# A deformable convolution and a top-2 mixture of experts on one core: the expert stage in two parts of 28 and 4 bands, with blocks of 128 rows

## The reference, cut to what matters

```
x = x + deformable_conv(layernorm_c(x))     # 3x3 taps, offsets and mask from a 3x3 convolution
t = tokens(x)                               # 4096 tokens of 128 channels
xf = layernorm(t)
logits = xf @ gate_w + gate_b               # 8 experts
probs = softmax(logits);  top2_vals, top2_idx = top_k(probs, 2)
for e in experts:
    h = gelu(xf @ W1[e] + b1[e])            # 128 -> 256
    y = h @ W2[e] + b2[e]                   # 256 -> 128
    out += weight of e for the token (0 if not chosen) * y
x = t + out
```

## Time and profile before

| what | us |
|---|---|
| median of 3 runs (lowest to highest) | 394.06 (393.71 to 394.44) |
| the profiled execution: its own time | 396.24 |
| its span, from the first to the last instruction | 394.4 |
| PE, PEld busy | 307.0, 261.2 |
| DVE, ACT, POOL busy | 224.6, 203.4, 217.8 |
| mean granted TensorE clock | 0.913 of full |

### The profile page before, as it was taken

The page is one execution under the profiler, slowest core; times in us unless marked ns, Lnnn a source line. Parts: engine busy times, 40 slices in busy tenths (PEclk is TensorE's granted clock), DMA queues, the critical chain, the costliest instruction groups (busy, mean ns, idle before and its releaser), DMA issues.

```text
span 394.4 us, 9789 instructions
## 1 busy us (share of the span) xinstructions
PE 307.0 (78%) x2395; PEld 261.2 (66%) x2395; DVE 224.6 (57%) x988; ACT 203.4 (52%) x526; POOL 217.8 (55%) x319
## 2 busy tenths in 40 slices
PE   0999599999999999999999984069889887885000
PEld 0365388888898888898888873048767676775000
DVE  2974347888888888888888775402122221222085
ACT  1254557667667766766766750324434443432053
POOL 5012232576776767777777545206777777777300
PEclk9999869999999999999999997559999999999555
DMA  8948822222222222222222100654768777771397
GB/s 212 272 131 239 318 75 85 84 97 101 88 97 93 97 89 91 96 93 91 92 92 96 53 28 28 167 168 156 231 202 252 222 229 237 234 227 63 94 316 229
DMA packets 50345, 57.83 MB, mean 147 GB/s; under 512 B 6892, under 2 KB 37999, under 8 KB 50320
## 3 DMA queue, kind: packets, MB, share of 16 engines
q1 hardware_dynamic: 43824, 48.12, 38.7%
q0 software_dynamic: 4544, 8.44, 6.6%
q10 hardware_dynamic: 1952, 0.99, 1.2%
HBM read 30.66 MB, written 14.97 MB: 116 GB/s over the span
## 4 chain that ended last, share of the span: by engine, by line
PE 51%; SPq 16%; issue 10%; ACT 8%; DMA 8%; POOL 2%; DVE 2%; ACTq 2%; POOLq 0%; DVEq 0%
PE bank L1367 18%; PE bank L1357 16%; ACT samp L765 7%; SPq L490 5%; PE bank L1272 5%; SPq L499 4%; SPq L505 3%; PE bank L1306 3%; DMA wide<-result 2%; DMA w_blk<-w_all 2%; POOL result L665 2%; PE bank L1284 2%; DMA result<-y,to 1%; PE bank L1478 1%; SPq L542 1%
## 5 line engine op out<-in xcount | busy, mean ns | idle before, releaser
L665 POOL DMA_INDIRECT result<-y,to x78 | 76.8, 985 | 41.9 <-DVE to L1215 23.0
L1367 PE MATMUL bank<-filt_sb,samp 128*128 128x128 f32 x576 | 77.0, 282 | 5.9 <-ACT samp L765 4.7
L1357 PE MATMUL bank<-S,xwin 100*128 100x144 f32 x512 | 79.8, 307 | 0.1
L604 POOL DMA_INDIRECT routed<-payload,slot x64 | 64.5, 1007 | 25.7 <-issue 15.0
L1367 PEld LDWEIGHTS bank<-filt_sb,samp 128*128 128x128 f32 x576 | 70.1, 194 | 11.2 <-ACT samp L765 9.8
L1357 PEld LDWEIGHTS bank<-S,xwin 100*128 100x128 f32 x512 | 69.4, 194 | 8.4 <-issue 7.3
L1223 DVE TENSOR_TENSOR y<-bank,w_blk 128x256 f32<-128x256 f32 x39 | 16.6, 425 | 79.9 <-PE bank L1487 76.8
L736 ACT ACTIVATE ysp<-bank 100x512 f32<-100x512 f32 (+1 forms) x96 | 46.7, 487 | 26.8 <-PE bank L1306 25.3
L932 DVE TENSOR_TENSOR S<-ysp,bank 100x512 f32<-100x512 f32 (+1 forms) x96 | 53.0, 553 | 9.8 <-ACT ysp L736 3.8
L765 ACT ACTIVATE samp<-bank 128x432 f32<-128x432 f32 (+1 forms) x96 | 47.2, 492 | 20.4 <-PE bank L1357 19.3
L1478 PE MATMUL bank<-rowsT,w_blk 128*128 128x256 f32 x156 | 45.0, 413 | 15.6 <-DMA w_blk<-w_all 13.7
(11 more groups left out here) (109 smaller groups left out, 433.8 us busy)
## 6 DMA issues: line engine op xcount, KB each, us to landing
w_blk<-w_all SPq DMA_DIRECT2D x39, 321.0 KB
xwin<-lines SPq DMA_DIRECT2D x64, 120.0 KB
xwin<-lines SPq DMA_DIRECT2D x32, 160.0 KB
rows_in<-routed SPq DMA_DIRECT2D x39, 129.0 KB, 2.6
wide<-result SPq DMA_DIRECT2D x16, 256.0 KB, 4.7
w_all<-in_experts SPq DMA_DIRECT2D x4, 642.0 KB, 7.5
out_tiles<-res SPq DMA_DIRECT2D x8, 256.0 KB, 4.6
wide<-in_x_rows SPq DMA_DIRECT2D x3, 512.0 KB, 9.2
```

Of the source, the lines that this page charges most:

```text
L604: nc.gpsimd.indirect_dma_start(routed, bass.IndirectOffsetOnAxis(slot[:, par, c2:c2 + 1], 0), payload[:, q, c2, :], None).then_inc((s.scat ...
L665: nc.gpsimd.indirect_dma_start(result, bass.IndirectOffsetOnAxis(to[:, slot, j:j + 1].bitcast(U32), 0), y[:, slot, j, :], None, bounds_che ...
L1357: last = nc.tensor.matmul(bank[5 + (par + g) % 2][:, i * TAPS * TT:(i + 1) * TAPS * TT], xwin[:, q, t, :], weights[:, t], start=True, stop ...
L1367: last = nc.tensor.matmul(bank[7][:, 0:C], samp[:, par, j, :], filt_sb[:, order[j], :], start=(j == 0), stop=(j == TAPS - 1))
```

## The change

The tokens are divided into two parts, the first 28 bands and the last 4. Each part has its own half of every expert's region in `routed`, its own running count (`seen`, `seen2`), its own plan and its own paddings.

- Blocks have 128 rows (`BLOCK = P`). Part 0 has at most 63 of them and part 1 at most 15, 78 in all, in a straight list without a loop. A send is now one indirect DMA for each block, with the destinations read from `rows_in` itself; `keep_dest` and `to` are gone.
- Part 0 is counted by PE in band 30's step and planned by DVE in the steps of bands 30 and 31 (`plan`, 14 links; the plan is computed with one block per partition and turned by two small matmuls, `turn_plan`). Part 1 is planned between the blocks 3 and 14.
- SP writes all paddings, those of part 0 before the first block, those of part 1 after block 26. It fetches eight block rows at a time. Rows have 16 slots and are loaded four blocks ahead of the weights.
- SP's weight transfer carries W1, b1 and b2 only (386 floats for each of 128 partitions instead of 642), into six slots. PE reads W2 where it lies, in `w_all`, at an address from the expert's number, which it has from packed words (`load_words`).
- The last bands' steps hold the first blocks' instructions already.
- `y_back` has a place of its own for each of the eight groups. A token's number is now its partition times 32 plus its band, so that a group is loaded back by one DMA with 2 KB pieces. SP issues the loads of the first seven groups behind its last weight transfer; ACT issues the eighth. DVE combines in place in `x1`.

```diff
-BLOCK = 256
+BLOCK = P
+SPLIT = 28
+PART_BANDS = (SPLIT, BANDS - SPLIT)
...
-W_UP = HID + HALVES
-WROW = W_UP + HALVES * C + C
-RING = 4
+W_B2 = HID + HALVES
+W_KEPT = W_B2 + C
+WROW = W_KEPT + HALVES * C
+RING = 6
+ROWS_AHEAD = 4
+ROWS = 16
...
+PACK, PACK_BITS = 8, 3
...
             def load_weights(i, row):
+                slot = i % RING
                 expert = nc.s_assert_within(row >> REGION_BITS, 0, EXPERTS - 1)
                 at_least(sp, s.y_done, i - (RING - 1))
-                sp.dma_start(w_blk[:, slot, :], w_all[:, expert, :]).then_inc(w_arrived[slot], 16)
+                sp.dma_start(w_blk[:, slot, :], w_all[:, expert, 0:W_KEPT]).then_inc(w_arrived[slot], 16)
+            def load_rows(i, row):
+                slot, uses = i % ROWS, i // ROWS
+                at_least(sp, sent[slot], 16 * uses)
+                sp.dma_start(rows_in[:, slot, :], routed[bass.ds(row, BLOCK), :]).then_inc(rows_arrived[slot], 16)
...
+            write_paddings(0)
+            sp.wait_ge(s.idle_written, 16)
             sp.wait_ge(s.experts_loaded, 16 * (EXPERTS // 2))
             sp.wait_ge(s.plan_ready, 1)
+            rows = []
+            for i in range(BLOCKS + ROWS_AHEAD):
+                if i < BLOCKS:
+                    part, at = int(i >= FIRST_BLOCKS), i % FIRST_BLOCKS
+                    if i == FIRST_BLOCKS:
+                        sp.wait_ge(s.plan_ready, 2)
+                    if at % PACK == 0:
+                        rows += first_rows(part, at)
+                    if at == 0:
+                        part_written(part)
+                    load_rows(i, rows[i])
+                if i >= ROWS_AHEAD:
+                    load_weights(i - ROWS_AHEAD, rows[i - ROWS_AHEAD])
+                if i == 26:
+                    write_paddings(1)
+            all_sent(sp, FIRST_BLOCKS)
+            for g in range(FIRST_BACKS):
                 load_back(g)
+            for g in range(BACKS):
+                if g == FIRST_BACKS:
+                    all_sent(sp, BLOCKS)
+                sp.wait_ge(s.out_ready, g + 1)
+                sp.dma_start(out[:, g * GB:(g + 1) * GB, :], x1[:, g * GB:(g + 1) * GB, :]).then_inc(s.stored, 16)
...
                 scatter(BANDS - 2, 0, 2)
+                send(0)
                 scatter(BANDS - 1, 1, 3)
...
+            for i in range(1, BLOCKS):
+                send(i)
...
+            for i in range(2, BLOCKS):
+                gelu(i)
+                if i + 2 < BLOCKS:
+                    evacuate_rows(i + 2)
+                if i == 12:
+                    act.wait_ge(s.exp_in, 1)
+                    nc.scalar.activation(e_all[:, :, :], e_all[:, :, :], ACT.Exp).then_inc(s.exp_out, 1)
+                    gelu_table(3)
...
+            for g in range(BACKS):
+                if g == FIRST_BACKS:
+                    all_sent(act, BLOCKS)
+                    for h in range(FIRST_BACKS, BACKS):
+                        act.dma_start(y_back(h), result[0:2 * P * BANDS, :].rearrange(
+                            "(c p g b) d -> g p c (b d)", c=2, p=P, b=GB)[h]).then_inc(back_arrived[h], 16)
...
+                    if known and b == SPLIT + 2:
+                        for link in range(6):
+                            plan(0, link)
+                    if known and b == SPLIT + 3:
+                        plan(0, PLAN_LINKS)
+                        plan(0, PLAN_LINKS + 1)
                     normalise(b - 1, other, (q + 3) % QUEUED)
...
+            def down(i, expert):
+                slot = i % RING
+                pe.wait_ge(s.h_ready, i * HALVES + HALVES)
+                for h in range(HALVES):
+                    last = nc.tensor.matmul(moe_bank[slot][:, 3 * BLOCK:4 * BLOCK], hid[:, slot, h, :],
+                                            w_all[:, expert, W_KEPT + h * C:W_KEPT + (h + 1) * C],
+                                            start=(h == 0), stop=(h == HALVES - 1))
+                last.then_inc(s.y_psum2, 1)
...
+            for i in range(3, BLOCKS):
+                if i == 12:
+                    turn_plan(1, BANDS)
+                if i == 40:
+                    experts_of += load_words(pe, mybir.EngineType.PE, 1, 0, SECOND_WORDS)
+                up(i)
+                if i + 2 < BLOCKS:
+                    transpose_rows(i + 2)
+                down(i - 1, experts_of[i - 1])
+            down(BLOCKS - 1, experts_of[BLOCKS - 1])
```

More of the change, by code:

```diff
@@ L327, in settle @@
             eng.sem_inc(s.settled, 1)
[L330 to L343, removed]
-                step(TURNS, place)
@@ new lines, in program, with y_back, all_sent @@
+        back_arrived = (s.back_0, s.back_1, s.back_2, s.back_3, s.back_4, s.back_5, s.back_6, s.back_7)
+        w_arrived = (s.w_in_0, s.w_in_1, s.w_in_2, s.w_in_3, s.w_in_4, s.w_in_5)
+        def y_back(g):
+            return y_first[:, g] if g < 4 else y_more[:, g - 4]
+        def all_sent(eng, blocks):
+            for slot in range(ROWS):
+                eng.wait_ge(sent[slot], 16 * len(range(slot, blocks, ROWS)))
+        PLAN_LINKS = 12
+        moe_bank = (bank[0], bank[1], bank[2], bank[3], bank[5], bank[6])
@@ L361, in program, with load_words @@
+        def load_words(eng, kind, part, first, end):
+            eng.wait_ge(s.experts_loaded, 16 * (EXPERTS // 2))
+            eng.wait_ge(s.words_ready, part + 1)
+            _, held = nc.values_load_multi_w_load_instructions(
+                words[0:1, part, first:end], engines=[kind], min_val=0, max_val=(1 << PACK * PACK_BITS) - 1)
+            return [(word >> PACK_BITS * at) & (EXPERTS - 1) for word in held for at in range(PACK)]
         x_arrived = (s.x_in_0, s.x_in_1, s.x_in_2, s.x_in_3)
@@ L369, in rows_of, with part_of @@
             return ap.rearrange("(one o) -> one o", one=1).broadcast_to([P, n])
-        def write_paddings(eng, kind, first, n):
-            _, rows = nc.values_load_multi_w_load_instructions(
-                pad_row[0:1, first:first + n], engines=[kind], min_val=0, max_val=(EXPERTS - 1) * REGION + P * BANDS)
-            for row in rows:
-                eng.dma_start(routed[bass.ds(row, BLOCK), :].rearrange("(p j) w -> p j w", j=PAD_RUN),
-                              padding_sb[:, :, :].bitcast(F32)).then_inc(s.pads_written, 16)
+        def part_of(b):
+            return 1 if isinstance(b, int) and b >= SPLIT else 0
         def is_far(eng):
@@ L847, in _ @@
[L847 to L857 removed]
+                evacuate_rows(0)
@@ L964, in _, with choose @@
             CHAIN = 6
-            def choose(b, par, link):
+            DVE_KIND = mybir.EngineType.DVE
+            def choose(b, par, link, part=None):
                 if no_band(b):
                     return
+                ranks = (seen, seen2)[part_of(b) if part is None else part]
                 if link == 0:
@@ L1122, in step @@
                         multiply(b, par, 2)
+                    if known and b == SPLIT + 3:
+                        for link in range(6, PLAN_LINKS):
+                            plan(0, link)
                     residual(b - 1, other, 0)
@@ L1231, in _ @@
[L1231 to L1248 removed]
+                finish(1)
@@ L1251, in _ @@
+            for g in range(BACKS):
+                combine(g)
         @block.tensor
```

613 lines of the change are left out of this document (317 added, 296 removed).

## The result

| | before | after |
|---|---|---|
| median (lowest to highest) | 394.25 (393.71 to 394.98, 4 runs) | 419.07 (416.96 to 420.26, 4 runs) |
| ratio of the runs, 95% interval | | 1.0622 [1.0574, 1.0671] |
| the profiled execution, its span | 396.24, 394.4 | 416.96, 415.2 |
| mean granted TensorE clock | 0.913 | 0.909 |

The change makes the kernel 6.2% slower: 24.8 us by the medians, 20.8 between the two spans. The forecast was 413.1 us in a range of 390 to 429.

A forecast was written before the change was run, and what follows sets the result against it. SP's instructions per block were taken as the bound. From the span of 394.4 us, start -13.4, SP's loop +50.8 and tail -18.3 gave 413.5; +1.84 and -2.18 made it 413.1 us, range 390 to 429.

The forecast's parts named there:

- SP's price for a pair: SP's block loop: one weight issue and one row issue per 128-row block cost 1.47 us, 78 times, 114.7 us.
- Fetches: SP's register loads of eight block rows: 3.0 us each, nine behind the first make 27 us (22 to 32).
- Paddings of part 1: SP writes all eight in its block loop after block 26: 7.0 us, or 9 at the earlier issue median.
- The start: SP's first row load comes at 242.0 us instead of 255.44, as part 0's counts are taken two bands earlier.
- The last weights: SP's last weight issue comes at 390.7 us, 37.4 later than the 353.3 of before.
- The tail: From the last weight issue to the span's end: 22.8 us, against 41.1 before.
- the last group's own load comes in time: In the tail: this 4.72 us load is ready, its blocks being sent some 10 us before DVE gets there.
- From span to median: Whole kernel: span 413.5 plus 1.84 around it, minus 2.18 for the profiled execution above the median, gives 413.1 us.
- Rival one: SP's loop: issues cost by size, SP stops being the bound; median 383 us, or 373 with POOL setting the pace; chance 0.15.
- Rival two, the clock: PE in the block loop: at the 1.2 GHz level it exceeds SP's 1.91 per block; median 440, half about 426; chance 0.10.
- SP's loop: SP from first row load to last weight issue: 148.7 us for 97.9 before, +50.8.

The follow-up runs named there:

- the double fetch: The kernel after, with each of the 10 fetches of row numbers into SP's registers done twice in a row: 443.47 us, ratio to before 1.1235.
- the extra issue: The kernel after, with one more SP DMA issue per block, copying the gate's 4 KB table into an unread spare tile: 452.71 us, ratio to before 1.1479.
- the fastest kernel: Not singled out in the text; the lowest are weights copied for six blocks only (373.9 us) and DVE copying weights (374.41 us, or 374.4 with two copies earlier).
- the kernel with the weights once: The kernel after, but SP copies expert weights only for the first six blocks, so results differ from the reference: 373.9 us, ratio to before 0.95.
- the first kernel with DVE's copies: The kernel after, but DVE copies W1, b1 and b2 into the slot three blocks ahead and SP issues only rows: 374.41 us, ratio to before 0.9483.

## Why the prediction was right

The mechanism, the sign and nearly all terms held; two sizes at the end were off, and some of the close agreement before them is luck. By its steps:

- **SP's price for a pair**, 1.47 us predicted: 1.46 to 1.48 inside a group, without a wait in it. The price of a weight issue was the same at 65, 193 and 321 KB. The parts are not those predicted: the row issue took 0.445 us where 0.38 was expected, and the steps between the issues came out shorter by as much.
- **Fetches**, 27 us for nine: from the first row load (241.78) to the last weight issue (390.28) are 148.5 us; less 78 x 1.47 = 114.7 and 7.2 for the paddings, 26.6 are left. Read one by one, the nine distances with a fetch in them are 3.98 to 4.49 us, 24.6 more than nine pairs, 2.7 each, as the double fetch gives by itself. The 3.0 had in it a longer load (0.81; 0.535 at the median after). The 2 us that are left are a balance: single long issues, such as 0.945 and 1.072, which the sum had not foreseen, less what the first rows and last weights save by being issued without a partner (0.83 for a weight issue alone). That the loop came out within 0.2 us of the forecast is luck; its terms were off by up to 2.4.
- **Paddings of part 1**, 7.0 us: 286.02 to 294.71 between two weight issues is 8.69, less 1.47 gives 7.2. These issues took 0.31 to 0.65 us where 0.38 was taken for each, and from one start to the next it was 0.55 at the mean ((293.15 - 289.31) / 7) instead of 0.53.
- **The start**, 242.0: 241.78. POOL's last scatter was indeed late (255.63 us for 249.14) and SP's distances show nothing of it; held back by 11.7 us, the start moved the end by 11.6.
- **The last weights**, 390.7: 390.28.
- **The tail**, 22.8: 415.2 - 390.28 = 24.9. DVE was free at 396.41 (6.1 us behind the weights, 5.3 predicted). Its seven groups took until 408.8, and then came the wait of 1.73 for the last group's load. The step that failed is "the last group's own load comes in time": the blocks were sent in time (the last send began at 398.36), but I left out that the load stands behind ACT's scaling of seven groups. ACT reached the seventh at 404.40, when that group's load had landed, so the eighth was issued at 405.01 and landed at 410.5, 1.7 us after DVE was free. I had followed the semaphore and not the order of instructions on the engine that issues.
- **From span to median**: 413.5 + 1.84 - 2.18 took the offset of one execution before for that of the kernel after. Before, the profiled execution was 2.18 above the median; after, it was the fastest of four, 2.11 below it. That is 4.3 of the 6.0 us between 413.1 and 419.07; the span itself was missed by 1.7. Which execution is profiled is chance, and the sum should not have used it.

Rival one (SP not the bound) is refuted by the transfer with a third of its bytes, which left the issue at 0.497, and by the extra issue, which added all of its 0.43 a block. Its figure for that world, 373 to 383 us, takes in where the kernels without SP's weight issues came out, 374, though by another way: there the issues were gone, not cheaper.

Rival two, the clock, is there and is covered. By stage the granted clock goes down to 0.80 and 0.83 of full in the loop, with PE busy for 11.05 of 20 and for 18.77 of 22 us (columns as in the earlier trace rows):

```profile
290.00:310.00 20.00, 11.05 (x68) 10.37 (x67) 2.04 (x7) 5.56 (x21) 7.12 (x8) 0.80 0.64 159
...
370.00:392.00 22.00, 18.77 (x126) 17.14 (x125) 4.07 (x14) 10.78 (x42) 12.86 (x14) 0.83 0.57 186
```

SP's fetches leave pauses on PE, and a stretch at the 1.2 GHz level follows most of them: PE took up work again at 307.4 us, and its granted clock was 0.50 from 309 to 312; it did so again at 318.4, and the clock was 0.50 from 320 to 322. Its blocks then take longer than SP's 1.47; further on in the group it is at 2.4 GHz again and catches up. The weight loads of `up` in one group:

```profile
310.62 0.97 PEld L1469 LDWEIGHTS bank<-rowsT,w_blk 128*128 128x128 f32 x4
...
312.50 0.53 PEld L1469 LDWEIGHTS bank<-rowsT,w_blk 128*128 128x128 f32 x4
...
313.50 0.53 PEld L1469 LDWEIGHTS bank<-rowsT,w_blk 128*128 128x128 f32 x4
```

1.88 us for a block at the low level (310.62 to 312.50), 1.00 at the high one. Eight blocks and a fetch give SP 14.3 us, in which PE has room for both. SP never waited for a y, and where SP was given more to do or started later (three experiments) the end moved by about as much: so the clock did not set the end. In the fastest kernel, where PE had no such pauses, the granted clock was 1.00 from 280 to 348 us.

Where the 20.8 us between the spans went: start -13.7 (255.44 to 241.78), SP's loop +50.6 (148.5 for 97.9), tail -16.2 (24.9 for 41.1).

## What to carry to other kernels

Count the instructions of the engine that only issues DMAs as carefully as those that compute: halving a block doubles its issues, and a pair of them here cost 1.47 us, with 65 KB of weights as with 193, more than the 1.29 of the send that was to be fed. When a queue of issues is the bound, move the copy to an engine with idle time (DVE, 0.40 us for 128 x 386 values) before moving anything in time; and for each load in the tail look at what stands before it in the program of the engine that issues it. The early start and the early return were worth 10 and 8 us here, and the 45 us of the weight issues outweighed both. Before two traces are compared by absolute times, look whether they already differ ahead of the edit; and count off whether a releaser that the chain names was really the last to be waited for.

## What the runs showed of the hardware that I had not expected

- A row issue took 0.333 us at the median when only row issues followed each other, and 0.445 when each stood behind a weight issue, with the same 64.5 KB; in the kernel after, those behind a fetch took 0.34 (318.71 us). The row of the kernel with the weights once (that of after stands above):

```profile
L516 SPq DMA_DIRECT2D rows_in<-routed x78: 332/333/1339, 241.8 to 338.9; - x78
```

  Why an issue costs 0.11 more behind one of another kind was not tested.
- POOL's indirect DMA took 0.98 us as a rule. While DVE combined groups, five or six sends in a row took 1.43 to 1.47, in each of the three kernels in which POOL sent that long beside it (352.79 us above, and the maxima of 1.474 and 1.472 by line). In the kernel after, where only two sends met a combine, it was 1.10 at most. DVE's combining alone does not explain it: in the first kernel with DVE's copies the sends at 348.56 and 349.84 us ran beside DVE's first group (from 348.07) and took 0.98. The slow ones cost about 3 us (six times 0.49) at the end of the fastest kernel. What they have in common was not tested.
- DVE's copies of 128 x 386 values did not slow those sends: the send at 301.89 us took 0.98 with a copy beside it from 302.13 to 302.49, and the median over all 78 was 0.983.
